# A wide edge pass: the last four row gathers of a block are tied to PE's third product of the same block

## The reference, cut to what matters

```python
msg_in = jnp.concatenate([nodes[row], nodes[col], edge_features], axis=-1)
messages = jax.nn.relu(msg_in @ mW1 + mb1) @ mW2 + mb2
aggregated = jax.ops.segment_sum(messages, col, num_segments=nodes.shape[0])
```

## Time and profile before

| what | value |
|---|---|
| median of 3 runs | 13255.19 us (13254.66 to 13275.64) |
| profiled execution, its own time | 13289.4 us |
| its span, first to last instruction | 13287.6 us |
| mean granted TensorE clock | 0.74 of full speed |
| PE busy | 7454.2 us (56%) |
| DVE busy | 6787.0 us (51%) |
| POOL busy | 6379.9 us (48%) |
| ACT busy | 2833.7 us (21%) |
| wide pass, 8600 to 13000 us: POOL, DVE, PE, ACT busy of 4400 us | 2698.5, 2137.6, 1673.7, 735.6 us |

### The profile page before, as it was taken

One profiled execution on the slowest core, in us unless ns is written; L12 is line 12 of the kernel. 1 busy time (PEld: TensorE's weight loads), 2 busy tenths in 40 slices (PEclk: granted clock), 3 DMA queues, 4 the chain that ended last, 5 costly groups with the idle time before them and its releaser, 6 DMA issues. The chain is left out here.

```text
span 13287.6 us, 144498 instructions
## 1 busy us (share of the span) xinstructions
PE 7454.2 (56%) x52956; PEld 5652.5 (43%) x52956; DVE 6787.0 (51%) x8156; ACT 2833.7 (21%) x2654; POOL 6379.9 (48%) x6717
## 2 busy tenths in 40 slices
PE   9755455555455454579999996333333333333335
PEld 4333333333333333369999995222222222222224
DVE  5466666666666666642222223444444444444445
ACT  4333333333333333320000001111111111111112
POOL 4456556565565656500000002666666666666664
PEclk9866776766767667789999997666666666666667
DMA  9722232222322223269979995333333333333332
GB/s 389 296 102 103 98 107 98 103 102 98 107 98 104 101 101 104 101 229 370 370 295 365 370 370 181 89 90 89 89 89 89 89 89 89 89 89 89 89 89 66
DMA packets 480426, 2020.11 MB, mean 152 GB/s; under 512 B 193465, under 2 KB 246136, under 8 KB 354776
## 3 DMA queue, kind: packets, MB, share of 16 engines
q1 hardware_dynamic: 205304, 1283.59, 27.6%
q0 software_dynamic: 206272, 317.25, 9.2%
q10 hardware_dynamic: 68768, 418.23, 8.6%
HBM read 1385.92 MB, written 632.61 MB: 152 GB/s over the span
## 5 line engine op out<-in xcount | busy, mean ns | idle before, releaser
L428 POOL DMA_INDIRECT big<-Yd,ix x3223 | 3041.5, 944 | 2062.7 <-PE ps L535 1088.5
L1296 POOL DMA_INDIRECT big<-Pd,mt x3223 | 3041.0, 944 | 1994.9 <-DVE ps L1325 962.8
L462 DVE TENSOR_TENSOR ring<-ps,vw 128x2940 bf16<-128x2940 f32 (+1 forms) x516 | 1726.3, 3345 | 1755.2 <-PE ps L529 1480.1
L527 PE MATMUL ps<-ring 128*128 128x490 bf16 x3223 | 1437.1, 542 | 2022.8 <-DVE ring L465 1334.6
L1325 DVE TENSOR_TENSOR ps<-ps,big 128x1024 f32<-128x1024 f32 x403 | 494.4, 1227 | 2533.2 <-remote 2512.7
L527 PEld LDWEIGHTS ps<-ring 128*128 128x128 bf16 x3223 | 417.7, 130 | 2831.7 <-issue 1621.4
L535 PE MATMUL ps<-big 128*65 128x128 f32 x6446 | 1125.6, 341 | 540.0 <-issue 539.5
L535 PEld LDWEIGHTS ps<-big 128*65 128x65 f32 x6446 | 1022.9, 181 | 636.8 <-issue 630.3
L1417 PE MATMUL ps<-qw,te 128*128 128x128 f32 x3216 | 697.0, 334 | 1016.8 <-issue 1012.6
L549 ACT ACTIVATE Z<-ps 128x1470 bf16<-128x1470 f32 (+1 forms) x584 | 800.1, 1399 | 1800.9 <-remote 792.6
L549 ACT ACTIVATE big<-ps 128x1470 bf16<-128x1470 f32 (+1 forms) x576 | 787.5, 1397 | 1731.3 <-remote 874.7
(11 more groups left out here) (215 smaller groups left out, 11552.3 us busy)
## 6 DMA issues: line engine op xcount, KB each, us to landing
Yd<-big SPq DMA_DIRECT2D x196, 1024.0 KB, 8.8
Aj<-Z SPq DMA_DIRECT2D x65, 3062.5 KB
big<-Aj SPq DMA_DIRECT2D x130, 1531.2 KB, 8.3
cb<-Aj ACTq DMA_DIRECT2D x130, 1531.2 KB, 8.4
Aj<-big SPq DMA_DIRECT2D x64, 3062.5 KB
cb<-Aj SPq DMA_DIRECT2D x128, 1531.2 KB, 8.3
Z<-Aj ACTq DMA_DIRECT2D x128, 1531.2 KB, 8.5
dr<-in_dstr SPq DMA_DIRECT2D x135, 1152.0 KB
```

Of the source, the lines that this page charges most:

```text
L428: e.indirect_dma_start(gv[j][:, k, 0:64], None, table, bass.IndirectOffsetOnAxis(ap=ix[j][:, k:k + 1], axis=0)).then_inc(sm[f"g{j}"], 16)
L462: nc.vector.tensor_tensor(one[r][:, 0:m, :], bc_t(iof, m, W * NT), bc_f(vw[j][:, k], m, W * NT), ALU.is_equal)
L527: nc.tensor.matmul(PS[q][:, 0:W * NT], olo[r][:, c, :], one[r][:, c, :], start=True, stop=False)
L1296: e.indirect_dma_start(gv[j][:, k, :], None, Pd, bass.IndirectOffsetOnAxis(ap=mt[j][:, k:k + 1], axis=0)).then_inc(sm[f"g{j}"], 16)
```

## The change

In POOL's turn, before the 21st gather (k = 20) of a block, POOL now waits until `p2` is b + 1, that is, until PE's third product of this same block is done. An increment of the `pool` semaphore follows, as after the waits at the turn's start; no engine waits on it. One more register is made per turn for the value. The first 20 gathers of a block and the last block (7 gathers) wait for nothing new. No other engine's code changes, and the number of gathers is the same.

```diff
                     e.wait_ge(sm[f"m{j}"], 16 * i + 16)
                     e.sem_inc(sm["pool"], 1)
-                    for k in range(KL if at(b, NB - 1) else K):
+                    last, n = at(b, NB - 1), reg(e, b + 1)
+                    for k in range(KL if last else K):
+                        if k == 20:
+                            e.wait_ge(sm["p2"], n)
+                            e.sem_inc(sm["pool"], 1)
                         e.indirect_dma_start(gv[j][:, k, :], None, Pd,
                                              bass.IndirectOffsetOnAxis(ap=mt[j][:, k:k + 1], axis=0)
                                              ).then_inc(sm[f"g{j}"], 16)
```

## The result

The changed kernel is slower: **13553.66 us** (13547.23 to 13564.5, 4 runs) against 13264.45 us (13254.66 to 13275.64, 4 runs) for the kernel before, ratio 1.0219 [1.0201, 1.0236], or +289 us. A later repetition (e11) gave 1.0223. The profiled execution has a span of 13547.0 us, at a mean clock of 0.741 (0.74 before).

The account below looks back on a forecast made before the run. Running gathers were taken to delay PE's updates and slow PE until about 4 us after POOL stops. 34.85 + 1.4 = 36.3 us a block against 36.98, x 133 = -90, +5 at the start: 13170 us; range 12985 to 13740.

Parts of the forecast that it names:

- the first rival: PE's issue between T + 4 and T + 24: flowing gathers keep PE slow, 40.5 us a block, 13730 us; chance 0.34.
- Does the wait bind?: POOL's 21st gather: yes, POOL will stand after 20 gathers in each block, so PE's updates can arrive.
- From p2 to the next T: From PE's third product seen, through four gathers, to the start of DVE's third gather-add (T): 10.55 us.
- From T to the stop: From the start of DVE's third gather-add (T) until POOL's 20 gathers of the next block end: 20.0 us.
- A recovery as long as before: After POOL stops, PE's updates arrive 3.93 to 4.09 us later, as in the kernel before.
- The transpose: PE's transpose of the last sum, now amid gathers: estimated 0.9 us late, putting 5 to 7 further matmuls behind the release.
- the rival of the stuck transpose: The transpose's update arrives only when POOL stops: 48.7 us a block, +1560, 14815 us; chance 0.05.
- The left-over of 1.4 us: PE's work still to run after POOL's release, per block: averages of 1.7 us (low clock) and 0.8 (high), taken as 1.4.
- What PE has left at T + 24: PE's matmuls not issued 24 us after DVE's third gather-add starts: the disputed term, taken as 1.4 us a block.
- a left-over of 0.1 us: Fast end of the prediction's own range for PE's remaining work per block: -272 us, 12985 us.
- 10 is nearer to 7: Gathers issued before SP's loads: with 10, PE was expected to run as after 7 (no stall), not 28 (stalled).
- quiet stretch: Time after SP issues its 1.5 MB when the gathers' queue moves no packets; claimed to let PE's first work through.

Follow-up runs that it names:

- e11: The changed kernel, unaltered, run again on another chip beside the kernel before: 13548.74 us, ratio 1.0223.
- e7: The changed kernel with SP's loads of targets and features cut to 128 of 3072 columns after the first two blocks: 13605.75 us.
- e2: The changed kernel with its wait before the 15th gather instead of the 21st: 13672.48 us, ratio 1.0311 to the kernel before.
- e5: The changed kernel with its wait before the 24th gather instead of the 21st: 13397.39 us against 13305.02 for the kernel before.
- e12: The changed kernel, but waiting for the first matmul of the previous block's third product: 13001.77 us, ratio 0.981 to the kernel before.
- e1: The changed kernel, but waiting for the previous block's third product instead of the same block's: 13122.32 us, ratio 0.9898 to the kernel before.
- e3: The changed kernel, with a block's first gather also waiting for the previous block's third gather-add: 13762.76 us against 13260.7 for the kernel before.
- e8: The kernel before with 12 gathers a block instead of 24: 11222.17 us against 13305.02.
- e4: The kernel before, gathering 64 of each row's 128 floats: 13253.22 us against 13260.7.
- e9: The wait for the first matmul of the previous block's third product, on the fast chip: 11290.73 us, ratio 0.9999 to the kernel before.
- e10: The wait for the previous block's third product, before the 15th gather, on the fast chip: 11291.24 us, ratio 0.9999 to the kernel before.

## Why the prediction was wrong

The forecast was 13170 us, faster by 0.6%; it came out slower by 2.2%, within the stated range of 12985 to 13740 and beside the first rival. By its own steps:

- **Does the wait bind?** Right, in all 134 blocks.
- **From p2 to the next T, 10.55 us.** Right: the third product ends at 10029.86 and T is 10040.42, 10.56 us later.
- **From T to the stop, 20.0 us.** Right, 19.9. A recovery as long as before: right too, 3.9 us from POOL's stop to PE's return.
- **The transpose, 0.9 us.** Nil. It ran at 10003.12, at once; the rival of the stuck transpose fell with it. The left-over of 1.4 us had been raised for it, so that the other reasons for a left-over were taken even lower.
- **What PE has left at T + 24, 1.4 us.** This failed, and it alone turned the sign. At T + 24 there were 22 matmuls left on average (20 to 23), where the prediction had nearly none in one block and 11 to 13 in the next. POOL's release came at T + 28.7 on average (19.95 of gathers, 9.57 of pause, less 0.86 of POOL's start), against 24.3 + 1.4 = 25.7. These 3.0 us x 133 are 399 us; -85 + 399 = +314, and the pass grew by 320.

Slips that moved none of this: 0.73 x 133 is 97 us, not 90; a left-over of 0.1 us gives -265, not -272; the third product of the earlier trace rows ends at 8548.76, not near 8547.6; and that PE's updates come about 4 us after POOL stops left out the one at 8553.46, amid the gathers.

The mis-sized term rested on one argument, "10 is nearer to 7": a quiet stretch behind SP's loads would let PE through if only 10 gathers had been issued ahead of it. The quiet stretch came. Three gathers were issued and none of the gathers' q0 moved in T + 2.6 to T + 5.6:

```profile
DMA packets 65, 0.80 MB, mean 266 GB/s; under 512 B 0, under 2 KB 0, under 8 KB 0
## 3 DMA queue, kind: packets, MB, share of 16 engines
q1 hardware_dynamic: 65, 0.80, 103.7%
issues: line engine op xcount, KB each, median us to landing
Z<-in_efT SPq DMA_DIRECT2D x1, 384.0 KB
big<-Pd,mt POOLq DMA_INDIRECT x3
```

PE stalled at T + 12.8 all the same, and cutting the loads (e7) changed nothing. What counted was that POOL was gathering already when PE's work began: the changed kernel's 8 gathers ahead of T are as bad as e2's 14, and the stall comes later with 5 or 2 (e5, e12) and later still with none (e1), so that 10 wasn't the near side of a threshold. The signal was in the rows that I read, the 42 matmuls after 28 gathers and the 73 after none; between them I should have drawn a line, which gives 73 - 31 x 10/28 = 62 out and some 11 left. That is at the rival's deciding point of 8 to 15, and still only half of what was measured: the slope is steep at its start and flat beyond 8.

The rival was right in its condition (gathers that are already flowing when SP's loads come keep PE slow) and wrong in its name: there was a quiet stretch, and PE stalled all the same. Its period, 40.5 us, was nearer to the measured 39.3 than mine, 36.3. The Trainium skill's rule in "DMA: Bandwidth & Descriptors", section "Queues, rings and completion order", is that an engine takes, in turn, a packet from each queue that has work. In these 3 us, with gathers in flight ahead of the loads, 65 packets of q1 stand beside none of q0, so the trace agrees only if the three issued gathers had no packets ready, which no row shows. The rule led to the right side, but by way of a missing quiet stretch, and the stretch was there.

Where did the removed `x2` pause go, 7.2 us a block? It went, as forecast. The 9.6 us in its place are 4 us of the same recovery, 4.7 us of PE's work that used to run under the gathers, and 0.8 us of POOL's start.

**What stays open.** That gathers ahead of T bring on PE's stall is shown by moving them. Why they do is not: whether PE's instructions or its semaphore updates queue up, and where, no row shows; that the one chip shows neither hold-back isn't explained. Whether a wait for a still earlier point of PE's work than e12's gains more wasn't tried.

## What to carry to other kernels

When two engines are in each other's way and a pause of one lets the other catch up, the pause costs its recovery plus the work still left, so place it where little is left. Letting the one go on before the other is through helped here too: the same wait, one block older and on a first matmul, was 4% faster than the changed kernel (ratios 0.981 and 1.022 on one chip). A time that depends on such a hold-back holds for the chip that it was measured on; run the kernel before on the same chip each time. And when two rows bracket a new case, interpolate at least, and ask what a threshold would rest on; here even the line gave half of what came.

## What the runs showed of the hardware

- On every chip but one, many updates of PE's semaphores that fall into a run of 24 gathers are seen only 3.8 to 4.2 us after its end (132 stops of the kernel before), even one that is 14 us old (e3), and PE's issue falls to one matmul per 2.1 to 2.8 us (the changed kernel). Others get through amid the gathers, 6 to 11 us late (the second product in one block of two of the kernel before) or at once (0.5 us from the transpose's end to its use in the changed kernel). The delay after the stop is 2.2 us after 12 gathers (e8), and with half the bytes 4.2 us instead of 4.0 (e4).
- On one chip neither occurs (e9, e10): 11292 us against 13257 to 13305 for the same kernel, with POOL's gathers at the same 1.25 us.
- 0.8 MB of a plain load passed in 3 us in which three gathers were issued and none moved a packet (the changed kernel, 10004 to 10007 us).
